# A 16-sequence decoder pair on one core: the masked layer's timetable starts four slots sooner, and GpSimd copies its head selections

## The reference, cut to what matters

```python
x = x + _L1_attn_ref(_layernorm(x), ...)              # 16 heads of 16, keys are the 100 rows
x = x + _L1_xattn_ref(_layernorm(x), ctx_1024, ctx_1024, mask, ...)   # 16 heads, 361 keys
x = x + _L1_ffn_ref(_layernorm(x), ...)
```

## Time and profile before

| | us |
|---|---|
| median of 3 runs | 1672.11 (1671.62 to 1685.03) |
| the profiled execution's own time | 1678.71 |
| its span, first to last instruction | 1676.6 |
| last self-attention probability unit of sequence 15 issued by PE | 1192.26 |
| first masked probability unit (sequence 0, slot 76) | 1217.87 |
| first unit of sequence 1 | 1235.69 |

### The profile page before, as it was taken

One profiled execution on the slowest core, in us unless ns is written; L12 is line 12 of the kernel. 1 busy time (PEld: TensorE's weight loads), 2 busy tenths in 40 slices (PEclk: granted clock), 3 DMA queues, 4 the chain that ended last, 5 costly groups with the idle time before them and its releaser, 6 DMA issues. The chain is left out here.

```text
span 1676.6 us, 30297 instructions
## 1 busy us (share of the span) xinstructions
PE 1492.7 (89%) x11672; PEld 1122.4 (67%) x11672; DVE 793.3 (47%) x2238; ACT 701.1 (42%) x1473; POOL 480.3 (29%) x428
## 2 busy tenths in 40 slices
PE   6999997899887999999999957988799999939997
PEld 4666664566665668888888834655467666629986
DVE  6577574657665422222222226776556666641111
ACT  3364464565656301222222233546655555512322
POOL 2123121111334445666666521111101111112332
PEclk9999998999999999999999978999899999969998
DMA  7342736697773215777777626357566767429996
GB/s 303 117 147 93 181 127 116 107 172 123 126 114 55 91 26 167 196 194 200 196 196 195 178 54 147 60 133 159 91 128 122 134 117 132 83 70 321 335 308 171
DMA packets 252439, 250.86 MB, mean 150 GB/s; under 512 B 116724, under 2 KB 226700, under 8 KB 246796
## 3 DMA queue, kind: packets, MB, share of 16 engines
q1 hardware_dynamic: 210316, 221.13, 51.7%
q0 software_dynamic: 41984, 27.84, 9.5%
HBM read 194.10 MB, written 54.58 MB: 148 GB/s over the span
## 5 line engine op out<-in xcount | busy, mean ns | idle before, releaser
L2831 PE MATMUL cross_ps_score<-cross_q,cross_k 128*128 128x250 f32 x1024 | 223.5, 376 | 0.8 <-DVE cross_q L3312 0.8
L2831 PEld LDWEIGHTS cross_ps_score<-cross_q,cross_k 128*128 128x128 f32 x1024 | 195.5, 191 | 23.9 <-DVE cross_q L3312 1.0
L3321 DVE TENSOR_TENSOR cross_prob<-cross_act_,cross_ps_score 128x250 f32<-128x250 f32 x128 | 53.2, 416 | 268.4 <-ACT cross_act_ L2999 268.4
L3415 POOL DMA_INDIRECT x_sum<-cross_ye,cross_token x64 | 128.6, 2010 | 80.6 <-ACT cross_ye L3005 68.5
L3026 DVE TENSOR_REDUCE cross_nmax<-cross_ps_score 100x2 f32<-100x722 f32 x128 | 111.9, 903 | 67.8 <-PE cross_ps_score L2579 64.3
L1745 ACT ACTIVATE layer_parts<-layer_ps_prob 128x400 f32<-128x400 f32 (+1 forms) x192 | 97.1, 509 | 107.9 <-PE layer_ps_prob L1561 105.8
L2861 ACT ACTIVATE cross_prob<-cross_ps_prob 128x400 f32<-128x400 f32 (+1 forms) x192 | 96.3, 508 | 94.9 <-PE cross_ps_prob L2612 93.2
L2999 ACT ACTIVATE cross_act_<-cross_ps_score 128x250 f32<-128x250 f32 x128 | 48.7, 380 | 167.7 <-PE cross_ps_score L2831 166.3
L2843 PE MATMUL cross_ps_prob<-cross_val,cross_prob 128*125 128x256 f32 x512 | 115.8, 379 | 0.0
L3405 POOL DMA_INDIRECT cross_xe<-ln_rows,cross_token x64 | 79.8, 1247 | 81.7 <-PE cross_ps_misc L2817 57.4
L2843 PEld LDWEIGHTS cross_ps_prob<-cross_val,cross_prob 128*125 128x125 f32 x512 | 93.5, 188 | 12.7
(11 more groups left out here) (471 smaller groups left out, 3117.1 us busy)
## 6 DMA issues: line engine op xcount, KB each, us to landing
packed_sb<-in_w SPq DMA_DIRECT2D x20, 1024.0 KB
experts_w<-in_w SPq DMA_DIRECT2D x20, 1024.0 KB
k_stack<-mixer_part SPq DMA_DIRECT2D x32, 541.5 KB, 4.1
cross_k<-in_wg SPq DMA_DIRECT2D x32, 512.0 KB
cross_k<-in_wu SPq DMA_DIRECT2D x32, 512.0 KB
cross_val<-in_wd SPq DMA_DIRECT2D x32, 512.0 KB
layer_stacks<-k_stack SPq DMA_DIRECT2D x30, 270.8 KB, 4.9
cross_k<-k_stack SPq DMA_DIRECT2D x25, 270.8 KB
```

What stands on the lines that cost most here:

```text
L2831: ins = nc.tensor.matmul(ps_pre[m][:, side, 0:CAP], w[s][:, k, m * P:(m + 1) * P], xt[s][:, k, :], start=(k == 0), stop=(k == KD - 1))
L3321: nc.vector.tensor_tensor(up[s][:, m, :], act_[:, m % 2, :], ps_pre[m][:, 1, 0:CAP], ALU.mult).then_inc(v_gated[m][s], 1)
L3415: g.indirect_dma_start(prog.x_sum, bass.IndirectOffsetOnAxis(token[:, 2 * e + t:2 * e + t + 1], 0), ye[s][:, t, :], None, compute_op=ALU.a ...
```

## The change

The masked timetable is laid four slots sooner: M_FROM is 72 in place of 76, so the lead-in has slots 60 to 71 and overlaps the whole step of sequence 15, and every later masked step begins four slots sooner with respect to self-attention's slots. The four copies of head selections leave ACT and go to POOL, in slot 69, behind `root4` of sequence 15 (slot 68), in the order `m_k[1]`, `m_k[1]`, `m_k[0]`, `m_k[0]`, each waited for before the next.

```diff
-    M_FROM = NQ * B + M_UNITS
+    M_FROM = NQ * B + M_UNITS - NQ
+    M_HEADS_AT = NQ * (B + 1) + 1
...
-                    if b == -1 and k in (0, 6):
-                        act.wait_ge(pe_prob, NQ * B)
-                        for h in range(2):
-                            m_select_heads(m_k[1 - k // 6], h, m_heads_set[1 - k // 6])
...
+                def m_select_heads(s, h):
+                    nc.gpsimd.tensor_copy(by_head(m_k[s], h, S2)[SHIFT_ROW:P],
+                                          prog.c("head_sel")[SHIFT_ROW:P, h * HH:(h + 1) * HH].unsqueeze(2)
+                                          .broadcast_to([32, HH, S2])).then_inc(m_heads_set[s], 1)
+                    g.wait_ge(m_heads_set[s], h + 1)
...
+                    if slot == M_HEADS_AT:
+                        g.wait_ge(pe_prob, NQ * B)
+                        for s in (1, 0):
+                            for h in range(2):
+                                m_select_heads(s, h)
```

## The result

The changed kernel takes 1681.72 us (median of 12 runs, 1675.25 to 1684.49), the kernel before 1671.86 in the runs beside it (1668.22 to 1685.03): a ratio of 1.0040, interval 1.0022 to 1.0058. The two medians are 9.9 us apart; by the ratio it is 6.7 us slower (3.7 to 9.7), where 2 us faster was forecast. Run once more, at another time and beside the kernel before again, it gave 1.0027 (1.0008 to 1.0046).

A forecast was written before the change was run, and what follows sets the result against it. TensorE was taken as the bound, busy 89%, with a hole at the seam between the attentions. First masked unit 1.7 us sooner and step 0 0.3 sooner gave -2.0 us: 1670.1, range 1664.5 to 1674.5.

The forecast's parts named there:

- The four slots: Seam: score units fill DVE's idle waits, 4.2 us won; with query projections moved, first masked unit at 1209.3 without holds.
- The copies' length: Head-selection copies on POOL: 2.59 us each, 10.5 us for four, from about 1205.8 to 1216.3, nothing late.
- What the copies do to DVE: Seam: POOL's copies hold CAST, TENSOR_TENSOR and TENSOR_SCALAR, costing 7.1 us; first masked unit at 1216.2, 1.7 us sooner than before.
- Step 0: First masked step: 17.1 us of PE work, 17.5 with small waits, against 17.8 before, so 0.3 sooner.
- Loads: SP's queue: sequence 1's two halves land by 1209 and 1212, needed from 1216.5 and 7 us later; hidden.
- Rival (d): Late keys: the first half would have to land 7 us later than worked out; 1672; chance 0.1 together with (e).
- the same exposure: Step 0: assumed 6.5 us at the low clock, as before; each us of PE work there costs up to 0.5.
- (a): Seam: copies hold no DVE instruction or only one; 6 to 8.6 us won, 1663.5 to 1666; chance 0.13.
- (b): Seam: copies hold two DVE instructions; -4.4 - 0.3 us, 1667.4; chance 0.2.
- (e): Seam doesn't shorten: slots 60 to 63 stretch as much as 64 to 67 save; 1672; chance 0.1 together with (d).
- (c): PE at 1.2 GHz through most of step 0 after a 5 us wait; 1674 likely, 1676 at worst; chance 0.15.

The follow-up runs named there:

- copies behind the rows: Changed kernel, with POOL waiting for normalise4 of sequence 15 before its four copies: ratio 1.0008 to the kernel before.
- the copies alone: Against the changed kernel, M_FROM stays at 76, so only the copies go to POOL: ratio 1.0018 to the kernel before.
- two of the experiments: Changed kernel with POOL's copies waiting for normalise4 of sequence 15 (1.0008), and with the copies kept on ACT, only the timetable moved (1.0053); ratios to the kernel before.
- the store moved: Changed kernel with group 3's store one slot later (79 in place of 78), behind sequence 2's first load: ratio 1.0018 to the kernel before.
- the best version: Changed kernel with the store one slot later, POOL's copies after normalise4 of sequence 15, m_k[0]'s two later still: 0.9955 and 0.9967 to the kernel before.

## Why the prediction was wrong, point by point

*The four slots.* Right within 1 us. Without the holds (copies behind the rows) the first unit is at 19.95 us, against 18.95 worked out (1209.3 less 1190.35). What the sum did not have: PE waits 3.37 us for the rows of sequence 14, and the projection behind them takes 2.03 us, at the low clock. (In passing, the stretch from 1188 to 1211 is 23.0 us long, not 22.5; nothing hangs on it.)

*The copies' length* on POOL: right, 10.54 us for four in the runs where no held VectorE instruction goes between them, against 10.5.

*What the copies do to DVE.* Right in kind, one term too large. The step took three holds, 7.1 us; there were two, 4.7. The TENSOR_SCALAR started at 1207.94, just where the second copy must end, and seems to have gone ahead of the third, with POOL waiting for it (the row gives the four copies as one, 10.70 us in place of 10.54, so this is read from the sum). With the copies alone it was held for 2.67, so tenths of a microsecond decide. The prediction called the TENSOR_SCALAR "held each time", but its own row gives a shortest of 402 ns, so one of those four was not held either. The low clock behind PE's wait, which the sum did not have, took 1.35 us (the turn 0.93, a values unit 2.04), and the four slots gave 1.0 less: 18.95 + 1.0 + 4.7 + 1.35 = 26.0, where 25.85 was forecast. That the first unit came out so near is luck, errors of opposite sign. The Trainium skill ("SBUF — State Buffer", section "Who interferes with whom") says that the instruction which issues first keeps the pair and the other fully blocks; both cases are in these rows, the CAST with 2.43 us for 16 elements a row and the slip of the TENSOR_SCALAR, as read above.

*Step 0.* 18.2 us, where 17.5 was forecast (17.8, 15.4 and 16.8 before). PE's work was 16.6 us, 17.1 forecast; the waits were 1.65 us, where 0.4 was allowed, most of them for DVE's maxima. The low clock lay only in its first 2 us, not in 6.5 (0.72 over 1208.4 to 1217.9).

*Loads.* Here the prediction failed. It said of the loads of sequence 1 that they were hidden, and they were; it never looked at those of sequence 2. The change laid slot 78's store and step 0's k = 6 into one slot, and of the queues that a moved step passes, SP's was followed for group 2 alone. The cost of these loads stood at nothing in the sum. The wait of 2.94 us (3.29 in the second profile, 2.18 and 2.91 in two of the experiments) and the clock behind it cost 4.3 to 4.6 us by sequence 2, and with the store moved the layer ends 5.2 to 5.7 sooner. Rival (d) named the mechanism, late keys, but for the wrong sequence, and priced it at 1672.

*The yardstick.* The second fault: step 0 with 6.5 us of low clock was taken as the kernel's own, and "the same exposure" was granted to both. Two more profiles of before show it at 15.4 and 16.8, and their first masked unit at 26.1 and 26.2, so against them the changed kernel's is hardly sooner. The layer was forecast at 291.2 (293.2 less 2.0) and ended at 296.6, which is the store's 5 to 6 us; the other 3 of the 9 between forecast and result are the dear profile.

*The rivals.* (a) is out: two instructions were held. (b) was right in its count, two held, and wrong in its time, since the first unit would have been at 23.1 us and not at 26.0. (e) is out as a mechanism: with the copies behind the rows DVE's gaps are filled and the first unit is 6 us sooner. (c), the low clock, has a share behind both waits and goes with them; by itself it isn't the cause. The change is under 1%, where nearly all of the chance lay.

## What to carry to other kernels

When one timetable is slid against another, list for every in-order queue, DMA issue included, the pairs of entries that change places or fall into one slot, to the end of the overlap and not only at the seam: a store that waits for late data must not stand ahead of a load that is due soon. A copy put on GpSimd "because it is idle" can hold VectorE's next instruction until it ends, however small that instruction is: here a CAST, a TENSOR_TENSOR and a TENSOR_SCALAR, all with their operands in SBUF, the on-chip memory that both engines read. So it belongs where VectorE's next such instruction is far, and in pieces. And one profile isn't a kernel: profile the unchanged kernel two or three times before a gain of a few microseconds is priced against it.

## What the runs showed that I had not expected

A CAST of 100x16 took 2.43 us and a TENSOR_TENSOR of that size 2.61 beside a GpSimd copy of 2.6, 14 and 15 times their 0.17. A wait of 2.94 us on PE cost 4.3 by the next sequence, one of 3.29 cost 4.6 (SP's first store of finished rows, L1356, is 59.2 and 59.6 us from the split's start, against 54.9 with the store behind), with the granted clock at 0.58 and 0.57 in the 4 us behind the first of them. The rest of the program behind the second layer, with the same code, took 193.0, 201.7 and 205.1 us in three executions of the kernel before, and 204.3 and 190.1 in two of the best version: what makes it so wide was not tried. The 162 matmuls of step 0 were busy 15.80 us in one execution and 13.38 in another, by the clock that was granted there.
